# Group normalisation with attention on one Trainium2 core: minus the group mean by a subtraction on VectorE in place of a TensorE product with a matrix of its own

## The reference, cut to what matters

```python
xg = x.reshape(B, N_GROUPS, C // N_GROUPS, H, W)
mu = xg.mean(axis=(2, 3, 4), keepdims=True)
var = xg.var(axis=(2, 3, 4), keepdims=True)
y = ((xg - mu) * jax.lax.rsqrt(var + EPS)).reshape(B, C, H, W)
y = y * gn_gamma[None, :, None, None] + gn_beta[None, :, None, None]
qkv = jnp.einsum('bchw,dc->bdhw', y, w_qkv) + b_qkv[None, :, None, None]
...
scores = jnp.einsum('bnc,bcm->bnm', q, k) * C ** (-0.5)
w = jax.nn.softmax(scores, axis=-1)
a = jnp.einsum('bnm,bmc->bnc', w, v)
...
return x + out
```

## Time and profile before

| | us |
|---|---|
| median of 3 runs | 136.11 |
| lowest, highest run | 136.02, 136.78 |
| the profiled execution | 135.91 |
| its span, first to last instruction | 134.1 |
| PE busy | 129.0 (96%) |
| DVE busy | 100.1 (75%) |
| ACT busy | 74.8 (56%) |
| POOL busy | 73.0 (54%) |

### The profile page before, as it was taken

One profiled execution on the slowest core, in us unless ns is written; L12 is line 12 of the kernel. 1 busy time (PEld: TensorE's weight loads), 2 busy tenths in 40 slices (PEclk: granted clock), 3 DMA queues, 4 the chain that ended last, 5 costly groups with the idle time before them and its releaser, 6 DMA issues.

```text
span 134.1 us, 1876 instructions
## 1 busy us (share of the span) xinstructions
PE 129.0 (96%) x579; PEld 91.1 (68%) x579; DVE 100.1 (75%) x191; ACT 74.8 (56%) x131; POOL 73.0 (54%) x78
## 2 busy tenths in 40 slices
PE   6999999999999999999999999999999999899991
PEld 6877687777777566666765656776665676558890
DVE  0598686999999999769788785698886826759121
ACT  3164768775588655656753284576732545868000
POOL 6133166589458877963386678933493355142600
PEclk9999999999999999999999999999999999999999
DMA  4950000000039808596799458963898299902111
GB/s 158 332 215 0 0 5 0 0 2 0 0 78 207 187 0 196 131 210 175 163 210 209 122 117 194 215 185 86 191 209 221 51 209 210 229 9 78 39 65 52
DMA packets 6874, 16.63 MB, mean 124 GB/s; under 512 B 1873, under 2 KB 2129, under 8 KB 6865
## 3 DMA queue, kind: packets, MB, share of 16 engines
q1 hardware_dynamic: 6576, 16.26, 49.4%
q10 hardware_dynamic: 288, 0.27, 0.6%
HBM read 2.36 MB, written 2.10 MB: 33 GB/s over the span
## 4 chain that ended last, share of the span: by engine, by line
PE 73%; DVE 9%; POOL 7%; issue 4%; DMA 2%; ACT 1%; POOLq 0%; DVEq 0%
PE mixed L847 22%; PE scores L793 8%; PE scores L794 8%; PE scores L796 8%; DVE scores L592 4%; PE turned L810 4%; POOL probs L334 4%; PE turned L740 3%; DVE crossed L619 3%; DMA xs<-in_x_dram 2%; PE mixed L849 2%; POOL y_lo L310 2%; PE mixed L740 1%; DVE stats L518 1%; PE mixed L844 1%
## 5 line engine op out<-in xcount | busy, mean ns | idle before, releaser
L334 POOL TENSOR_SCALAR probs<-probs,inv_sum 128x1024 f32<-128x1024 f32 x32 | 35.9, 1122 | 42.0 <-DVE inv_sum L597 41.9
L592 DVE TENSOR_SCALAR_CACHE_REDUCE scores<-scores,key_bias 128x1024 f32<-128x1024 f32 x31 | 40.0, 1289 | 11.5 <-PE scores L796 11.5
L421 ACT ACTIVATE probs<-scores,neg_max 128x1024 f32<-128x1024 f32 x32 | 35.7, 1116 | 20.0 <-DVE scores L592 19.2
L847 PE MATMUL mixed<-crossed,v 128*128 128x512 f32 x84 | 39.5, 592 | 0.0
L793 PE MATMUL scores<-y_hi,z_hi 128*128 128x512 f32 x62 | 34.5, 557 | 0.1
L619 DVE STREAM_TRANSPOSE crossed<-probs 128x1024 f32<-128x1024 f32 x24 | 29.8, 1242 | 1.4 <-POOL probs L334 1.2
L794 PE MATMUL scores<-y_lo,z_hi 128*128 128x512 f32 x62 | 24.4, 394 | 0.0
L847 PEld LDWEIGHTS mixed<-crossed,v 128*128 128x128 f32 x84 | 15.1, 190 | 11.0 <-issue 10.1
L796 PE MATMUL scores<-y_hi,z_lo 128*128 128x512 f32 x62 | 19.3, 392 | 0.0
L793 PEld LDWEIGHTS scores<-y_hi,z_hi 128*128 128x128 f32 x62 | 11.7, 189 | 8.5 <-issue 5.7
L794 PEld LDWEIGHTS scores<-y_lo,z_hi 128*128 128x128 f32 x62 | 11.7, 189 | 7.0 <-issue 5.5
(11 more groups left out here) (159 smaller groups left out, 179.5 us busy)
## 6 DMA issues: line engine op xcount, KB each, us to landing
crossed<-crossed SPq DMA_DIRECT2D x92, 128.0 KB, 2.3
out_dram<-result SPq DMA_DIRECT2D x7, 256.0 KB, 2.4
xs<-in_x_dram SPq DMA_DIRECT2D x2, 512.0 KB, 6.7
xs<-in_x_dram SPq DMA_DIRECT2D x3, 256.0 KB, 4.8
xs<-in_x_dram ACTq DMA_DIRECT2D x1, 256.0 KB, 3.3
ws<-in_weights_dram SPq DMA_DIRECT2D x1, 256.0 KB, 3.6
out_dram<-result SPq DMA_DIRECT2D x2, 128.0 KB, 1.9
vecs<-in_vectors_dram ACTq DMA_DIRECT2D x1, 3.0 KB, 3.8
```

What stands on the lines that cost most here:

```text
L334: pool.tensor_scalar(probs[:, i % RING, :], probs[:, i % RING, :], inv_sum[:, i:i + 1], 1.0, ALU.mult, ALU.mult).then_inc(s_probs, 1)
L421: act.activation(probs[:, i % RING, :], scores[:, i % 2, :], ACT.Exp, bias=neg_max[:, i:i + 1], scale=-1.0, accum_out=row_sum[:, i:i + 1]) ...
L592: dve.tensor_scalar(scores[:, i % 2, :], scores[:, i % 2, :], key_bias[:, b % 2, i:i + 1], None, ALU.subtract, ALU.min, accum_out=neg_max[ ...
L847: mm = pe.matmul(bank, v[:, b % 2, k, :], at, start=first, stop=final)
```

## The change

`minus_mean` and its PSUM column go, and with them one of the two products in `group_means`. DVE makes minus the group mean itself: the deviation is the channel mean less the group mean, so deviation less channel mean is minus the group mean. The new `negated_means` writes it to `negated_mean` in SBUF for all four batches; for batches 2 and 3 it takes the place of the copy. `coefficients` reads it there. PE waits for the subtraction where it is about to write into the bank that holds the deviation.

```diff
@@ pool
-            pool.tensor_scalar(minus_mean[:, :], group_mean[:, :], -1.0, None, ALU.mult).then_inc(s_const, 1)
@@ vector
-            def channel_spreads(lo, hi, matmuls, sums):
-                dve.wait_ge(s_gmean, matmuls)
+            def channel_spreads(lo, hi, sums):
+                dve.wait_ge(s_gmean, hi)
...
+            def negated_means(lo, hi, sums):
+
+                for b in range(lo, hi):
+                    dve.tensor_tensor(negated_mean[:, b:b + 1], sums[:, DEV + b:DEV + b + 1], mean_var[:, b, 0:1],
+                                      ALU.subtract).then_inc(s_negated, 1)
...
-            def coefficients(lo, hi, n, minus_means):
+            def coefficients(lo, hi, n):
                 dve.wait_ge(s_rstd, n)
-                dve.wait_ge(s_gmean, 2 * n)
+                dve.wait_ge(s_negated, hi)
...
                 if job == V1 and b + 1 < BATCHES:
-                    channel_spreads(b + 1, b + 2, 2 * (b + 2), bank)
-                    dve.tensor_copy(negated_mean[:, b + 1:b + 2],
-                                    bank[:, MINUS_MEAN + b + 1:MINUS_MEAN + b + 2]).then_inc(s_negated, 1)
+                    channel_spreads(b + 1, b + 2, bank)
+                    negated_means(b + 1, b + 2, bank)
...
-            channel_spreads(0, 1, 1, mixed[:, 1, :])
+            channel_spreads(0, 1, mixed[:, 1, :])
             variances(0, 1, 1, mixed[:, 1, :])
+            negated_means(0, 1, mixed[:, 1, :])
             half_stats(1, 0)
...
             maximum(0, 0)
-            channel_spreads(1, 2, 4, mixed[:, 0, :])
+            channel_spreads(1, 2, mixed[:, 0, :])
+            negated_means(1, 2, mixed[:, 0, :])
             maximum(0, 1)
@@ tensor
                 pe.matmul(sums[:, DEV + lo:DEV + hi], centring[:, :], mean_var[:, lo:hi, 0],
                           start=True, stop=True).then_inc(s_gmean, 1)
-                pe.matmul(minus_means[:, MINUS_MEAN + lo:MINUS_MEAN + hi], minus_mean[:, :],
-                          mean_var[:, lo:hi, 0], start=True, stop=True).then_inc(s_gmean, 1)
...
-                    pe.wait_ge(s_negated, b - 1)
+                    pe.wait_ge(s_negated, b + 1)
...
-            pe.wait_ge(s_const, 7 + GROUPS)
+            pe.wait_ge(s_const, 6 + GROUPS)
...
+            pe.wait_ge(s_negated, 1)
             pe.wait_ge(s_norm, 1)
...
             block_scores(0, 1)
+            pe.wait_ge(s_negated, 2)
             group_variances(1, 2, mixed[:, 0, :])
```

More of the change, by code:

```diff
@@ L81, in attention_kernel @@
         group_mean = sb("group_mean", [128, 128])
-        minus_mean = sb("minus_mean", [128, 128])
         minus_half = sb("minus_half", [128, BATCHES])
@@ L128, in attention_kernel @@
         mixed = ps("mixed", [128, 2, HALF])
-        DEV, MINUS_MEAN, VARIANCE = 400, 408, 416
+        DEV, VARIANCE = 400, 416
         setup = scores[:, 1, :]
@@ L544, in coefficients @@
                 for b in range(lo, hi):
-                    dve.tensor_scalar(norm_b[:, b:b + 1], minus_means[:, b - lo:b - lo + 1], norm_a[:, b:b + 1], BETA,
+                    dve.tensor_scalar(norm_b[:, b:b + 1], negated_mean[:, b:b + 1], norm_a[:, b:b + 1], BETA,
                                       ALU.mult, ALU.add).then_inc(s_norm, 1)
@@ L645, in _ @@
             channel_stats(0, 1)
-            channel_spreads(0, 1, 1, mixed[:, 1, :])
+            channel_spreads(0, 1, mixed[:, 1, :])
             variances(0, 1, 1, mixed[:, 1, :])
+            negated_means(0, 1, mixed[:, 1, :])
             half_stats(1, 0)
             dve.wait_ge(s_vecs, 16)
-            coefficients(0, 1, 1, mixed[:, 0, MINUS_MEAN:MINUS_MEAN + 1])
+            coefficients(0, 1, 1)
             dve.wait_ge(s_norm, 1)
@@ L695, in _ @@
                     if b == 0 and i == 0:
-                        coefficients(1, 2, 2, mixed[:, 0, MINUS_MEAN + 1:MINUS_MEAN + 2])
+                        coefficients(1, 2, 2)
                     if not swapped(BLOCKS * b + i):
@@ L714, in _ @@
                     if 0 < b < BATCHES - 1 and i == 1:
-                        dve.wait_ge(s_negated, b)
-                        coefficients(b + 1, b + 2, b + 2, negated_mean[:, b + 1:b + 2])
+                        coefficients(b + 1, b + 2, b + 2)
             tails_of_pair(dve, 1)
@@ L724, in _, with group_means @@
         def _(pe):
-            def group_means(lo, hi, sums, minus_means):
+            def group_means(lo, hi, sums):
                 pe.wait_ge(s_means, hi)
@@ L763, in projection @@
                     if job == V1 and b + 1 < BATCHES:
-                        group_means(b + 1, b + 2, bank, bank)
+                        group_means(b + 1, b + 2, bank)
                     if job == V2 and b + 1 < BATCHES:
@@ L880, in _ @@
             pe.transpose(setup[:, SET_W + C:SET_W + 2 * C], WK_T, ident[:, :]).then_inc(s_w_turned, 1)
-            group_means(0, 1, mixed[:, 1, :], mixed[:, 0, :])
+            group_means(0, 1, mixed[:, 1, :])
             keep_warm(1)
@@ L920, in _ @@
             pe.matmul(to[1], z_hi[:, 0, first], y_lo[:, 0, halves[1]], start=False, stop=True).then_inc(s_scores, 1)
-            group_means(1, 2, mixed[:, 0, :], mixed[:, 0, :])
+            group_means(1, 2, mixed[:, 0, :])
             pe.wait_ge(s_setup, 5)
```

## The result

| | before | after |
|---|---|---|
| median of the runs, us | 136.50 (10 runs) | 135.80 (10 runs) |
| lowest, highest, us | 136.02, 136.87 | 135.57, 136.03 |
| the profiled execution, us | 135.91 | 135.78 |
| its span, us | 134.1 | 134.0 |
| PE instructions | 579 | 571 |

The account below looks back on a forecast made before the run. PE was taken to bound the kernel (busy 96% of the span), with DVE also full from 23.4 to 58.3 us. Savings 0.00 + 0.22 + 0.13 + 0.22 = 0.57 us from 136.11 gave 135.54 us, range 135.05 to 136.15.

Parts of the forecast that it names:

- Price of one product: In PE's chain of waits, the pair of mean products costs 0.45 us and one of it 0.22 us.
- Batch 1: Product at 12.19 us goes with PE full on both sides; everything up to 23.4 us follows PE, saving 0.22 us.
- Batch 2: Product at 34.52 us goes while DVE is full; ACT starts 0.16 us earlier, subtraction costs 0.03, saving 0.13 us.
- Batch 3: Product at 60.06 us goes where PE is full and the other engines wait for it; saving 0.22 us.
- The head: Batch 0: PE waited for DVE's spread and the added subtraction is covered before `norm_a`; saving 0 us.
- Busy time: Over the whole profile, PE's busy time falls by about 0.9 us, with 8 instructions fewer.
- Rival 1: All three products of batches 1 to 3 pay in full, plus 0.05 in the head: 0.71 us, 135.40; chance 0.18.
- Rival 2: DVE takes back batch 2's saving at 40.88 us: sum 0.38 us, 135.73; chance 0.16.
- rival 3: DVE runs its small instructions one behind the other, delaying `norm_a` 0.09 to 0.17: sum 0.42 us, 135.69; chance 0.09.
- Rival 4: Less PE work in the head lets the clock drop to 1.2 GHz; 137.5 us for 2 us of work; chance 0.03.
- the drain rule: On DVE, the next op does not start until the pipeline has emptied; cited as speaking against the change.

Follow-up runs that it names:

- the kernel of batch 1 alone: Change made for batch 1 only, product kept for batches 0, 2 and 3, against the kernel before: 136.14 against 136.25 us, ratio 0.9987; profiled execution 138.82 us.

## Why the prediction was right

**Price of one product: right.** 0.22 us was read from the chain; the exponential of block 0 comes 0.22 to 0.24 earlier in all four executions of after.

**Batch 1: right.** Saving 0.22, and PE's extra wait for the subtraction cost nothing that the end shows. The wait was real: in the profile of after the weights of the variance product were loaded at 14.90 us, 6.92 behind `norm_a` where 7.07 stood, so 0.15 earlier and not 0.22, and PE had the rest back with block 2's first weights (16.00 us, 8.02 behind `norm_a` in place of 8.24), ahead of which it had been idle in both kernels. The shift was whole at block 8 (0.18 to 0.26 over the four), so the stretch in which DVE is full passed it on.

**Batch 2: right, 0.15 to 0.17 in place of 0.13.** The limit was the one named: ACT had been 0.20 us behind DVE's maximum and is 0.04 behind it now. I had charged 0.03 for a subtraction longer than the copy; they are equally long, and the sum without it is 0.16.

**Batch 3: right.** 0.16 to 0.23 more by block 17 in place of 0.22.

**The head: the term 0 was right where PE was at full speed, the check offered for it was wrong.** The prediction said `norm_a` "starts within 0.05 of 7.46" and that the prediction fails if the span of the head moves by more than 0.1. It moved by 0.52. I had read the head of one execution as the kernel's. The term holds where PE was at full speed by the time of the mean product and no transfer was late: 2.27 to 2.29 us from the start of the aggregation to `norm_a`, with the product or without. Over the 14 profiled executions `norm_a` starts between 7.46 and 8.56, and three causes were shown: when PE comes to full speed, when x arrives, when batch 1's first half arrives. Kernels that keep the head's product have the same spread (7.46, 7.52, 7.88, 8.56) as those without it, and it is larger than the gain. That is why a comparison here needs ten runs of each kernel and more.

**Busy time: wrong for this pair of profiles.** I forecast 0.9 us less of PE busy; it was equal, because products at half speed last longer. The two profiles of after in which full speed came by 5.3 us have 128.5 and 128.4 us, against 129.0 and 129.3 in the two of before: 0.5 to 0.9 less. Busy time is not work.

**Rival 1** (0.71) cannot be excluded by the medians (0.70, 0.40 and 0.71 us by the three ratios), but the exponentials decide: batch 2 paid 0.15 to 0.17, not 0.22. That the medians average slightly more than 0.57 may come from executions with a late clock, in which the product of batch 0 lay in the way, for about 0.3 us as one profile shows; that is not shown, and how often it happens was not measured.

**Rival 2** fell with the step at block 9, **rival 3** with the doubled subtraction. **Rival 4** did not decide the result, but the row I held against it was no evidence. The granted clock of 1.00 over the first 12 us stood there too in executions whose products ran at half speed, and in the very profile from which I read it the products ran at half speed until 4.4 us; so "the level of 2.4 GHz in all four" stretches was a misreading of the first. The mechanism is real at this place: with one warming product less, 5 of 12 executions have a mean granted clock of 0.987 or less, and 2 more took about 138 us. Of 34 executions of the full change one was above 137.5 us (137.83, clock 0.987), of 101 of the kernel before none (the highest took 137.18); that is too few to say that the change brought the kernel nearer to the edge, and a kernel with the head of before had one too.

## What to carry to other kernels

A product with one column cost its two weight loads here, 0.22 us wherever PE is full, and a small instruction on another engine that reads what is there already cost 0.06 us where that engine is full and nothing that could be seen in the head. But a saving in a stretch where a second engine is full is worth only that engine's idle time at the place where it waits, directly or through a third engine, for the first. When one profile is set beside another, fix a common event behind the noisy start and compare distances from there: that resolved 0.1 us where the medians of ten runs scattered by 0.3. Products that do nothing may carry the clock, so a product taken away where PE has gaps should be judged by the whole distribution of runs, not by a median.

## What the runs showed of the hardware that was not expected

PE's rate in the first microseconds is not what the record of the granted clock says. In the profile of the kernel of batch 1 alone:

```profile
10.00:11.00 1.00, 1.00 (x5) 1.00 (x6) 0.96 (x3) 0.39 (x2) 0.00 (x0) 1.00 0.00 0
12.00:13.00 1.00, 1.00 (x4) 0.78 (x5) 0.28 (x2) 0.76 (x2) 0.00 (x0) 1.00 0.00 0
```

The granted clock reads 1.00 throughout, while the starts of PE's products of 384 and 512 columns were 0.39 us apart on average (five of them, 12.00 to 13.57) and then 0.24 for products of 512 columns at full speed (13.88, 14.12, 14.36). Where the clock fell after having been up, the record shows 0.50. The record seems to hold changes only, with 1.00 in front of the first; what is shown is that a 1.00 ahead of the first full-speed product cannot be trusted.

Full speed, read from the starts of the passes (0.21 us apart before it, 0.11 behind), came between 3.9 and 4.7 us in six of the 14 profiled executions, at 5.2 to 5.4 in two, between 6.0 and 6.7 in five, and once after 13.6. The first eight products are the same in all of them, and begin at 1.04 us. Small DVE instructions of 0.14 to 0.16 us start 0.06 to 0.08 apart, also a subtraction that reads PSUM. Two subtractions in a row in the head cost no more than one. So the drain rule, as the prediction took it from the Trainium skill ("VectorE: DVE Perf Modes", section "The DRAIN you can't avoid"), does not hold for these instructions. The same section says that a next op that is not held starts earlier, which the prediction left out; the spacing measured here agrees with that sentence.
